# Expert tables, residual additions and row transposes spread over rounds; a search constant made in the preparation; two xT roundings put between mixed fills

## The reference, cut to what matters

```
x = x + xattn(layernorm(x), ctx)            # x: 2 x 1024 x 256, 16 heads, 64 keys
n = layernorm(x);  scores = (layernorm(n)*g + b) @ centroids.T        # 2048 x 8
for e in range(8):                          # balanced_assignment
    s = where(taken, -inf, scores[:, e]);  idx[e] = top_k(s, 256);  taken[idx[e]] = True
for e in range(8):
    r = n[idx[e]]                           # 256 rows of 256
    h = gelu((layernorm(r)*g + b) @ w1[e] + b1[e]) @ w2[e] + b2[e]
    out[idx[e]] = r + h                     # and x is added in the end
```

## Time and profile before

| what | value |
|---|---|
| median of 3 runs (lowest, highest) | 344.44 us (343.03, 345.68) |
| the profiled execution, whole time | 346.77 us |
| its span, first to last instruction | 344.6 us |
| mean granted TensorE clock | 0.93 |
| busy PE / PEld / DVE / ACT / POOL | 291.2 / 256.0 / 219.5 / 144.7 / 177.6 us |
| chain that ended last, by engine | PE 64%, DVE 13%, DMA 9%, issue 5%, POOL 5%, ACT 2% |

### The profile page before, as it was taken

The page is one execution under the profiler, slowest core; times in us unless marked ns, Lnnn a source line. Parts: engine busy times, 40 slices in busy tenths (PEclk is TensorE's granted clock), DMA queues, the critical chain, the costliest instruction groups (busy, mean ns, idle before and its releaser), DMA issues.

```text
span 344.6 us, 6499 instructions
## 1 busy us (share of the span) xinstructions
PE 291.2 (85%) x2066; PEld 256.0 (74%) x2066; DVE 219.5 (64%) x749; ACT 144.7 (42%) x265; POOL 177.6 (52%) x240
## 2 busy tenths in 40 slices
PE   8999799999999999998312379989989899899991
PEld 4999688989999899987201267777778687778890
DVE  0689898888878888784288666767676765120000
ACT  1466365455456554554400245353535353333320
POOL 8000533456665566545103655676767677885611
PEclk9999999999999999999655559999999999989997
DMA  7991006901000010001100232372718181806000
GB/s 275 346 390 26 2 0 245 363 34 64 30 30 30 30 61 30 30 33 61 61 0 0 66 120 61 81 257 64 274 43 289 35 288 42 314 2 210 34 11 20
DMA packets 21623, 37.50 MB, mean 109 GB/s; under 512 B 2400, under 2 KB 14944, under 8 KB 21216
## 3 DMA queue, kind: packets, MB, share of 16 engines
q1 hardware_dynamic: 19040, 30.89, 25.5%
q0 software_dynamic: 2560, 6.31, 6.0%
HBM read 30.90 MB, written 6.29 MB: 108 GB/s over the span
## 4 chain that ended last, share of the span: by engine, by line
PE 64%; DVE 13%; DMA 9%; issue 5%; POOL 5%; ACT 2%; DVEq 0%; POOLq 0%; ACTq 0%; SPq 0%
PE pair L886 55%; DMA G<-rows_scratch,idx 9%; PE pair L969 4%; DVE cmpb L750 3%; POOL G L414 2%; PE pair L936 2%; DVE pair L783 1%; POOL out_dram L445 1%; PE pair L1076 1%; PE pair L1041 1%; PE pair L998 1%; POOL w1p L424 1%; DVE wneg L600 1%; DVE G L790 1%; DVE ok L770 1%
## 5 line engine op out<-in xcount | busy, mean ns | idle before, releaser
L886 PE MATMUL pair<-w2s,hT 128*128 128x256 f32 x256 | 62.3, 394 | 0.0
L886 PE MATMUL pair<-yT,w1p 128*128 128x256 f32 x384 | 55.4, 297 | 0.0
L370 POOL TENSOR_TENSOR pr<-pr,rs 128x1024 f32<-128x1024 f32 x16 | 31.6, 1977 | 42.1 <-DVE rs L691 42.1
L886 PE MATMUL pair<-Bm,pT 128*128 (+1 forms) x384 | 50.0, 285 | 2.3 <-DVE pT L684 2.3
L886 PEld LDWEIGHTS pair<-w2s,hT 128*128 128x128 f32 x256 | 47.2, 195 | 6.2
L562 ACT ACTIVATE hT<-pair,b1s 128x256 f32<-128x256 f32 x64 | 26.8, 470 | 56.9 <-PE pair L886 56.6
L886 PEld LDWEIGHTS pair<-yT,w1p 128*128 128x128 f32 x384 | 50.2, 198 | 0.4
L886 PE MATMUL pair<-Am,xTp 128*128 (+1 forms) x192 | 48.7, 402 | 2.0 <-POOL xTp L358 2.0
L886 PEld LDWEIGHTS pair<-Bm,pT 128*128 128x128 f32 x384 | 47.0, 188 | 2.7 <-issue 2.7
L886 PEld LDWEIGHTS pair<-Am,xTp 128*128 128x128 f32 x192 | 34.9, 188 | 9.7 <-DVE Bm L594 2.4
L424 POOL TENSOR_TENSOR w1p<-w1s,w1p 128x512 fp32r<-128x512 f32 x32 | 40.0, 1274 | 0.2
(11 more groups left out here) (131 smaller groups left out, 525.1 us busy)
## 6 DMA issues: line engine op xcount, KB each, us to landing
w1s<-w_dram SPq DMA_DIRECT2D x8, 1024.0 KB
w2s<-w_dram SPq DMA_DIRECT2D x8, 1024.0 KB
rows_scratch<-row SPq DMA_DIRECT2D x16, 256.0 KB, 2.0
xs<-x_dram SPq DMA_DIRECT2D x1, 2048.0 KB, 17.1
xTs<-xT_dram SPq DMA_DIRECT2D x1, 2048.0 KB, 18.8
wk_s<-wk_dram SPq DMA_DIRECT2D x1, 1024.0 KB, 5.2
wv_s<-wv_dram SPq DMA_DIRECT2D x1, 1024.0 KB, 7.4
wqT_s<-wqT_dram SPq DMA_DIRECT2D x2, 512.0 KB, 8.8
```

The costliest lines, as they stand in the source:

```text
L370: pool_mul = nc.gpsimd.tensor_tensor(p4, p4, rs[:, v, :].unsqueeze(1).unsqueeze(3).to_broadcast([P, KG, H, K8]), ALU.mult)
L886: return nc.tensor.matmul(out_, l, r, start=start, stop=stop)
```

## The change

Six edits:
- `exp_r` is made by ACT in the preparation, ahead of fill 20, and no longer behind the stored rows.
- ACT rounds the `xTp` of tiles 0 and 1 between the mixed fills 40 and 41; steps -1 and 0 of its attention loop no longer do.
- DVE makes `Hoh` in round 1 (was 0) and `Loh` in round 2 (was 1).
- `final(k-3, 1)` moves from round 0 to round 3, ahead of `indices(u)`.
- TensorE's `rows` takes one half in round 6 and the other in round 7; `e_gT` counts halves, and ACT waits for both.
- A new function `keep_busy` issues BUSY = 3 matmuls of 512 columns on `ones_b` into bank 1 at the end of rounds 3 to 7 of slot k = 1: 15 in all.

Nothing else is computed, and SP's and POOL's own orders stay.

```diff
-WARM = 12
+WARM, BUSY = 12, 3
...
@@ ACT
+                if f == 20:
+                    act.wait_ge(s_in["cst"], 16)
+                    nc.scalar.activation(exp_r[:], expand, ACT.Copy).then_inc(r_init, 1)
+                if f == MIXED + 5:
+                    act.wait_ge(s_in["xT"], 16)
+                    for t in range(2):
+                        x_high(t, t)
                 if f >= MIXED:
                     mixed_high(f)
...
-            act.wait_ge(s_in["xT"], 16)
-
             def attn(s, u):
                 t = s + 1
-                if live(t):
-                    v = par(t, u, -1)
-
+                if live(t) and not (isinstance(t, int) and t < 2):
                     wait(act, s_lg, t - 1)
-                    nc.scalar.activation(xTp[:, 0, v, :].rearrange("p (c n) -> p c n", c=CC), xTs[:, :, ds(t * P, P)],
-                                         ACT.Copy).then_inc(s_xTh, 1)
+                    x_high(t, par(t, u, -1))
...
-                act.wait_ge(e_gT, e + 1)
+                act.wait_ge(e_gT, ST * (e + 1))
...
-            act.wait_ge(s_in["cst"], 16)
             act.wait_ge(s_in["small"], 64)
             act.wait_ge(s_sc, T)
             for v in range(2):
                 act.wait_ge(s_row[v], 16 * T // 2)
-            nc.scalar.activation(exp_r[:], expand, ACT.Copy).then_inc(r_init, 1)
@@ DVE
                         if r == 0:
                             slots(u)
                             halves(u)
+                        if r == 1:
                             one_hot(u, 1, Hoh, r_hoh)
-                        if r == 1:
+                        if r == 2:
                             one_hot(u, 0, Loh, r_loh)
-                        if r == 3:
-                            indices(u)
-                    if r == 0 and 0 <= k - 3 < E:
+                    if r == 3 and 0 <= k - 3 < E:
                         final(k - 3, 1)
+                    if r == 3 and 0 <= u < E:
+                        indices(u)
@@ TensorE
-            def rows(e):
+            def rows(e, a):
...
+            def keep_busy():
+
+                for _ in range(BUSY):
+                    mm(bank[1][:], ones_b[:, 0:P], ones_b[:], True, True)
...
-                        if r == 6:
-                            rows(u)
+                        if r in (6, 7):
+                            rows(u, r - 6)
+                    if k == 1 and r >= 3:
+                        keep_busy()
```

More of the change, by code:

```diff
@@ L471, in mixed_high, with x_high @@
                 nc.scalar.activation(mixed(f, 0), fill_bank(f)[:], ACT.Copy).then_inc(s_evA, 1)
+            def x_high(t, v):
+                nc.scalar.activation(xTp[:, 0, v, :].rearrange("p (c n) -> p c n", c=CC), xTs[:, :, ds(t * P, P)],
+                                     ACT.Copy).then_inc(s_xTh, 1)
             def centre(h):
@@ L1066, in spread @@
                 mm(bank[3][:, 32:32 + LO], exp_r[:], Rt[:], True, True).then_inc(r_Rx, 1)
[L1068 removed]
+            def rows(e, a):
                 b = e % GB
[L1071 removed]
+                if e > 0 and a == 0:
                     pe.wait_ge(e_yT, 4 * e)
[L1073 to L1077 removed]
+                pe.wait_ge(e_g[ST * b + a], 16 * (e // GB + 1))
+                for c in range(CC):
+                    last = nc.tensor.transpose(bank[0][:, c * CAP + a * P:c * CAP + (a + 1) * P],
+                                               G[:, b, a, c * P:(c + 1) * P], ident)
                 last.then_inc(e_gT, 1)
+            def keep_busy():
+                for _ in range(BUSY):
+                    mm(bank[1][:], ones_b[:, 0:P], ones_b[:], True, True)
             def up(e, f):
```

6 lines of the change are left out of this document (removed).

## The result

| | before | after |
|---|---|---|
| median (lowest, highest), same chip | 345.06 us (343.03, 346.44), 4 runs | 329.95 us (329.59, 330.23), 4 runs |
| profiled execution, whole time | 346.77 us | 330.23 us |
| its span | 344.6 us | 328.1 us |
| mean granted TensorE clock | 0.93 | 0.959 |

The ratio is 0.9566 with a 95% interval of 0.9525 to 0.9606: faster by 4.3%, or 15.0 us of 345. The prediction was 332.3 us with a range of 328.5 to 336.0. The sign and the range held, the time came out 2.4 us lower. Among the runs of the experiments one of before (495.24 us) and one of e11 (738.89 us) stood far out, and are left out everywhere.

A forecast was written before the change was run, and what follows sets the result against it. TensorE was taken to bound the kernel, losing time to waits and a low clock. Terms 1.95 + 3.3 + 3.5 + 1.3 + 0.6 + 0.8 + 0.7 = 12.15, taken from the median 344.44, gave 332.3 us; range 328.5 to 336.0.

The forecast's parts named there:

- Attention start: Start of the attention: with ACT's roundings moved ahead, TensorE's 1.99 us wait for POOL's rest of xTp goes; gain 1.95.
- search start: Start of the search: with exp_r made early, the first transposes wait only for M, near 167.7 instead of 171.04; gain 3.3.
- Slots 3 to 6: Compare and second-half waits go, waits of 0.3 for Loh and 0.45 for the first half come; gain 0.87 a slot, 3.5.
- Slots 7 and 8: Slot 7 keeps its first-half wait and gains only the second's 0.3; slot 8's 1.01 goes whole; gain 1.3.
- Slots 1 and 2 and the filling: Slot 1 gains 0.6 net of filling, slot 2 0.8 from its gather, and the clock 0.7 of 2.4.
- the clock holds from slot 1 through the blocks: Rival: no clock fall before slot 2's blocks, adding 1.7 in slot 2 and 0.5 in slot 1; 330.1 us, chance 0.23.
- the forecast's case: Before or in slot 2's first block the clock, raised in slot 1, falls again and returns sooner; 332.3 us, chance 0.45.
- A first block of 1.68 us: Sign in slot 2: this length, instead of a cold block's 2.90, would make the step on the clock wrong.
- the cost of the filling in slot 1: Slot 1: 15 matmuls fit in rounds 3 to 5 but delay total 7 and the ranks; taken as 0.5.
- The filling never raises the clock: Rival, slots 1 and 2: the 0.7 is gone and slot 1 pays 1.5, not 0.5; 334.0 us, chance 0.12.
- The slots don't shorten: Rival: the gather lands 0.9 later than reckoned and round 6's wait takes all that is saved; 335.8 us, chance 0.14.
- Slower than before: Rival, slots 2 to 6: round 6's wait grows to 2 us and the clock falls behind it; 348.8 us, chance 0.02.

The follow-up runs named there:

- e11: e9 with Hoh and Loh a round later in slot 1 alone, plus e10's filling in all rounds of slots 0 and 1; 326.79 us, ratio 0.9504.
- e2: The kernel after with ACT's copy of exp_r put back behind the stored rows; 333.75 us, ratio 0.9669.
- e5: The kernel after with ACT's first two roundings of xT put back at the start of the attention; 332.71 us, ratio 0.9669.
- e12: The kernel before with only the two moves on ACT (exp_r and the first two xT roundings); 337.00 us, ratio to before 0.9796.
- e4: The kernel after with Hoh back in round 0 and Loh in round 1, final left in round 3; 328.05 us, ratio 0.9512.
- e6: The kernel after with final(k - 3, 1) back in round 0, the tables left as they are; 332.98 us, ratio 0.9701.
- e7: The kernel after with filling matmuls only in rounds 3 to 5 of slot 1; 332.11 us, ratio 0.9676.
- e8: The kernel after with both tables in round 1, Loh right behind Hoh; 329.19 us, ratio 0.9574.
- e1: The kernel after without the 15 filling matmuls of slot 1; 331.75 us, ratio 0.9617.
- e3: The kernel after with both halves of the row transposes in round 6 again; 340.43 us, ratio 0.9886.
- e9: e4 with seven filling matmuls in slot 7, ahead of round 6's transposes; 329.12 us, ratio 0.9561.
- e10: The kernel after with three filling matmuls in every round of slots 0 and 1; 328.60 us, ratio 0.9563.

## Why the prediction was right or wrong

- **Attention start, 1.95, and search start, 3.3: right.** 5.5 together in the traces; e2 and e5 bring the two waits back at full length (3.9 and 2.3 ahead of the search), e12 alone has 4.9 of it.
- **Slots 3 to 6, 0.87 each: right in every step, with some luck in what it is measured against.** Count 1 without a wait, tokens 0.37 (0.3), first half 0.65 and 0.45 to 0.49 (0.45), second half none, the gather released by POOL's own queue, spacing 16.76 (16.8). The step that wasn't seen is in before: 0.5 of each 17.6 was a late end of the tokens, not the waits that were counted. Against e12's slots, without it, the change of the slots is worth 0.4 each. How many of before's unprofiled executions had it isn't recorded. After is not open to that loss: its gather waits for the scatters until 7.99 us into the slot, later than before's late `idx` at 7.69. Nor does the forecast's sum say which edit is worth what: with `Hoh` left in round 0 the slots are 0.9 shorter still (e4).
- **Slots 7 and 8, 1.3: wrong in both terms.** Slot 7 gained 2.3 instead of 0.3, since the clock did not fall behind the 1.75 us; that fall had cost before 1.7, and I took it for given as long as a wait of that kind stayed. The traces of before, e4, e6 and e12 show that the length of the wait doesn't decide it alone: two falls at 2.01 and 1.93, none at 2.01 and 2.01. Slot 8 gained 0.5 instead of 1.0: its first half, now waited for in its own round, is 0.66 late.
- **Slots 1 and 2 and the filling, 2.1: mis-sized, 4.6 in the trace.** The forecast was that the clock rises in slot 1 and falls again before or in the first block. The rival, *the clock holds from slot 1 through the blocks*, is what the profiled execution shows. The other three executions of after have mean clocks of 0.955 to 0.959; a fall like e7's, from 193.9 to 197.3 us, takes about 0.005 off the mean, an estimate from those times, so that they can't be sorted into the two cases. A first block of 1.68 us was the sign that would make this step wrong, and it took 1.67. What I held against the rival, the fall at 303 us, came behind a stretch in which TensorE did nothing; behind the filling it works half of the time, but that is no safe rule: in e2, e5, e7, e8 and e11 the forecast's case happened, with slot 2 0.8 to 1.2 us longer. Even then slot 2 is 0.8 to 1.1 us shorter than e1's, which is more than the 0.7 allotted, as the clock is back within the second block. The other part that was mis-sized is the cost of the filling in slot 1, put at 0.5: without it (e1) the slot took 14.17 us, with it 13.93 in after, and 14.49 and 14.59 in e2 and e8, where the clock rose later.
- **The hit on a time is luck in part.** The rival's 330.1 is the measured time to 0.2 us, and the forecast's 332.3 is 2.4 off. But slot 7's 2.0 more and slot 8's 0.5 less were foreseen by neither, and 1.4 of the traces' 16.5 doesn't appear in the medians. The range of 7.5 us holds both cases of the clock, so that it did not test which of them would come.
- **The other rivals.** *The filling never raises the clock* did not happen in any trace; without filling (e1) slot 2 is 1.9 longer. The prediction's price for a cold filling matmul, 0.426 us at 1.2 GHz, was read from the warm-up, where the profile's own clock row says 1.00; it holds all the same, three at a granted clock of 0.50 in after took 1.28 from 186.97 to the next count. *The slots don't shorten* fell with 16.76. *Slower than before*, the wait of round 6 with a fall behind it, did not happen in after; with the transposes joined, e3 shows both at once in slot 5, waits of 0.53 and 0.94 and a fall, and is still 1.1% faster than before (0.9821 to 0.9951).
- **Against which time.** The sum was taken from the median, which assumed that the profiled execution of before differs from it in nothing that the change touches. The traces differ by 16.5, the medians by 15.1. The late ends and the fall in slot 7 are in the profiled execution; that they are missing in some of the others would explain the difference, but wasn't recorded.

What is open: what makes the end of a small matmul group reach another engine 0.8 to 1.3 us late, slot after slot in one kernel and not in another, and what decides whether the clock falls in slot 7 or at the end of slot 1. Both were seen, neither was produced at will.

## What to carry to other kernels

When an operation is moved to a later round to free an engine, follow it through the slowest queue that waits for it: here `Hoh`'s move took 0.33 us of waiting for the compare away and made the gather 1.0 later in the slot through POOL's queue, while `final`, which only the second scatter waits for, could be moved without TensorE waiting for it. Split a wait for several transfers, so that each stands where its data is due: in the kernel after that was worth 1.2 us in each of slots 3 to 6. And price a stage against more than one trace of near-identical kernels before giving its whole length to the waits that it shows.

## What was not expected of the hardware

- **Ends that arrive late.** The same instructions, at the same clock, signalled 0.26 or 1.03 us behind the start of a count (e4 and e9), 0.70 or 2.00 us behind the start of the tokens (e12 and before), the same way in most slots of a trace. It cost 0.5 to 0.75 us in each of these, more than most of the edits here, and nothing where a later wait took it up (after, 0.62 to 0.66 behind count 5).
- **The clock's answer to the same wait.** In slot 7, 1.75, 1.86, 1.84, 2.01 and 2.01 us of idle left it at 2.4 GHz (after, e1, e2, e6, e12); behind 2.01 and 1.93 it was down to 1.2 within 1.3 us (before, e4).
- **The clock under a half load.** With three filling matmuls a round, which fill the round at 1.2 GHz and 0.81 us of its 1.33 at 2.4, it held through slot 1 in after, fell at the end of slot 1 in e8 with the same filling, and fell in e10's slot 0, behind a selection in which TensorE had 0.24 us of work in the window of 178 us.
